# A gated decoder stack on one core: shared last feed-forward product, token shift by transfers, one barrier, gathers dealt out between scatters, merged end

## What is computed

```python
x = x + tanh(g_xattn[0]) * L0_xattn(layernorm(x), ctx)
x = x + tanh(g_ffn[0])   * L0_ffn(layernorm(x))
x = x + tanh(g_xattn[1]) * L1_xattn(layernorm(x), ctx, ctx)
x = x + tanh(g_ffn[1])   * L1_ffn(layernorm(x))

# one of the two layers of L0_ffn (HID = 682)
x = x + local_attention(shift_token(x)) @ wo
h = shift_token(x)                 # second half of the channels from the token before
h = (h - mean) / sqrt(var + 1e-5) * lg + lb
a, g = split(h @ w1 + b1)          # 682 values, 682 gates
x = x + (a * gelu(g)) @ w2 + b2

# L1_ffn, after the router has chosen idx[e], 128 tokens for each expert e
y = gelu(xe @ fc1[e].T + b) @ fc2[e].T + b2
output[idx] += y * gate;  sums[idx] += gate
output = where(sums > 0, output / sums, output)
```

## Time and profile before

| | us |
|---|---|
| median of 3 runs | 2104.79 |
| lowest, highest | 2097.73, 2105.27 |
| the profiled execution's own time | 2111.36 |
| its span, first to last instruction | 2109.6 |
| TensorE busy in it | 1819.5 (86%) |
| VectorE busy | 1278.1 (61%) |
| ScalarE busy | 1036.2 (49%) |
| GpSimd busy | 695.0 (33%) |
| mean granted clock of TensorE | 0.957 of 2.4 GHz |

### The profile page before, as it was taken

The page is one execution under the profiler, slowest core; times in us unless marked ns, Lnnn a source line. Parts: engine busy times, 40 slices in busy tenths (PEclk is TensorE's granted clock), DMA queues, the critical chain, the costliest instruction groups (busy, mean ns, idle before and its releaser), DMA issues. The chain is left out here.

```text
span 2109.6 us, 32684 instructions
## 1 busy us (share of the span) xinstructions
PE 1819.5 (86%) x11580; PEld 1199.6 (57%) x11580; DVE 1278.1 (61%) x2729; ACT 1036.2 (49%) x2194; POOL 695.0 (33%) x997
## 2 busy tenths in 40 slices
PE   6988888888799797997999989999998998870894
PEld 3455555555567466674666655466666554550794
DVE  5478888888623584233787842268876334967112
ACT  3488888888521263212767621157674111540221
POOL 0022223232332444323555521045554112450321
PEclk9999999999899999998999999999999999995897
DMA  3441111110000200021000020020000000046694
GB/s 117 158 122 41 41 42 41 41 42 2 1 0 1 60 1 1 1 61 43 1 1 1 1 62 1 0 57 1 1 1 1 0 0 16 1 146 139 198 310 134
DMA packets 99138, 99.65 MB, mean 47 GB/s; under 512 B 33740, under 2 KB 83232, under 8 KB 98848
## 3 DMA queue, kind: packets, MB, share of 16 engines
q1 hardware_dynamic: 95904, 93.21, 15.0%
q0 software_dynamic: 3072, 4.34, 1.1%
HBM read 80.60 MB, written 16.92 MB: 46 GB/s over the span
## 5 line engine op out<-in xcount | busy, mean ns | idle before, releaser
L585 DVE TENSOR_REDUCE negmax<-sps 128x1 f32<-128x1024 f32 x256 | 308.3, 1215 | 36.2 <-PE sps L530 31.0
L629 ACT ACTIVATE prob<-sps,negmax 128x1024 f32<-128x1024 f32 x256 | 287.6, 1124 | 22.2 <-DVE negmax L585 17.8
L539 PE MATMUL sps<-ident,prob 128*128 128x128 f32 x1152 | 178.3, 283 | 57.5 <-ACT prob L629 56.6
L539 PEld LDWEIGHTS sps<-ident,prob 128*128 128x128 f32 x1152 | 134.7, 143 | 142.8 <-ACT prob L629 123.0
L1491 POOL TENSOR_TENSOR la_pr<-la_pr,la_ri 128x512 f32<-128x512 f32 x128 | 157.1, 1255 | 164.2 <-DVE la_ri L1553 164.2
L674 POOL TENSOR_TENSOR probT<-probT,after 128x128 f32<-128x128 f32 x256 | 116.6, 455 | 268.4 <-DVE probT L593 192.6
L1738 ACT ACTIVATE la_pr<-la_pr,la_nx 128x256 f32<-128x256 f32 x256 | 126.3, 494 | 128.6 <-DVE la_nx L1594 128.6
L530 PE MATMUL sps<-ks,qs 128*128 128x512 f16 x512 | 162.5, 393 | 11.1 <-DVE ores L605 4.4
L1922 PE MATMUL la_bs<-lf_zT,lfw 128*128 128x512 f32 (+1 forms) x384 | 168.7, 594 | 0.0
L1501 POOL TENSOR_TENSOR la_qs<-la_qn,ores 128x256 f32<-128x256 f32 x128 | 113.6, 918 | 89.1 <-DVE la_qn L1607 89.1
L638 ACT COPY probT<-sps 128x512 f32<-128x512 f32 (+1 forms) x192 | 101.8, 530 | 40.5 <-PE sps L539 40.5
(11 more groups left out here) (384 smaller groups left out, 3808.7 us busy)
## 6 DMA issues: line engine op xcount, KB each, us to landing
w1e<-in_fc_T SPq DMA_DIRECT2D x16, 1024.0 KB, 5.6
w2e<-in_fc_T SPq DMA_DIRECT2D x16, 1024.0 KB, 8.6
qs<-q_parts SPq DMA_DIRECT2D x128, 64.0 KB, 1.9
ks<-k_parts SPq DMA_DIRECT2D x128, 64.0 KB, 2.0
q_parts<-parts SPq DMA_DIRECT2D x8, 512.0 KB, 3.7
k_parts<-parts SPq DMA_DIRECT2D x8, 512.0 KB, 3.6
ores<-in_L_ffn_wqkv SPq DMA_DIRECT2D x2, 1536.0 KB, 6.3
lfw<-in_L_ffn_w SPq DMA_DIRECT2D x2, 1364.0 KB
```

What stands on the lines that cost most here:

```text
L539: mm = pe.transpose(slots[n % 4][:, at * P:(at + 1) * P], prob[:, n % 3, t * P:(t + 1) * P], ident[:])
L585: dve.tensor_reduce(negmax[:, n % 4:n % 4 + 1], slots[n % 4][:], X, ALU.max, negate=True).then_inc(s.max_done, 1)
L629: act.activation(prob[:, n % 3, :], slots[n % 4][:], ACT.Exp, bias=negmax[:, n % 4:n % 4 + 1], accum_out=rowsum[:, tile % 2, n % QUAD:n % ...
```

## The change

1. **Last product shared.** The 42 gates and 42 values left over come from one matrix of 128 columns (values in columns 0 to 41, gates in 64 to 105, zeros between), so that chunk 5 takes two matmuls, not four. The gelu reads partitions 64 to 105 and writes 0 to 41. The weights come in 13 transfers, not 10, two of them narrow.
2. **Shift by transfers.** `late` is gone from TensorE, with `shift` and `carry`. For each group SyncE copies the half rows of x one partition down into a new SBUF tile `xs`, with two transfers after the attention has updated the group's tiles. VectorE reads `xs` from SBUF where it read PSUM. Two rows of `xs` are blanked by GpSimd at the start of the block, and VectorE waits for that before its first work (`tables`).
3. **One barrier, one release.** The four calls of `signals` end in one barrier; the five of `release` become one.
4. **Gathers dealt out.** GpSimd issues six gathers, and then one behind each of the first ten scatters.
5. **Merged end.** The end has no block: SyncE reads `mixed` as soon as the last scatter has landed, into the space of the expert weights. The divisor takes one instruction, and of each group's four result tiles the last goes to ScalarE (product) and GpSimd (sum). The semaphores are cleared behind it.

```diff
-            w1 = sb(ph + "w1", [P, KD, 2 * HID], F32, c)
+            w1 = sb(ph + "w1", [P, KD, 2 * (NF - 1) * P + P], F32, c)
...
+                for n in range(2):
+                    sp.dma_start(w1[:, :, n * full:(n + 1) * full], w1_rows[:, :, n * HID:n * HID + full]).then_inc(sem, 16)
+                with nc.allow_non_contiguous_dma(reason="the last channels of values and gates"):
+                    for n in range(2):
+                        at = 2 * full + n * P // 2
+                        sp.dma_start(w1[:, :, at:at + HID - full], w1_rows[:, :, n * HID + full:(n + 1) * HID]).then_inc(sem, 16)
...
+                            for g in range(G):
+                                t0, t1 = g * J, g * J + J
+                                sp.wait_ge(sa[l].x_done, t1)
+                                sp.dma_start(xs[1:P, t0:t1, :], x0res[0:P - 1, t0:t1, HALF:D]).then_inc(late[g], 16)
+                                if t0 % TPB == 0:
+                                    t0 += 1
+                                sp.dma_start(xs[0:1, t0:t1, :], x0res[P - 1:P, t0 - 1:t1 - 1, HALF:D]).then_inc(late[g], 16)
...
+                        for b in range(B):
+                            pool.memset(xs[0:1, b * TPB, :], 0.0).then_inc(sf[0].first_blank, 1)
...
-                                dve.tensor_scalar(z[:, j, HALF:D], tps(g)[0][:, j * P:(j + 1) * P], mom[:, j, 0:1], rs[:, j:j + 1],
+                                dve.tensor_scalar(z[:, j, HALF:D], xs[:, g * J + j, :], mom[:, j, 0:1], rs[:, j:j + 1],
...
+                            if l == 0:
+                                dve.wait_ge(w.first_blank, B)
                             tables(l)
...
-                            for dst, off in ((pg[f % 2], HID), (pa[f % 2], 0)):
+                            full = (NF - 1) * P
+                            pairs = ((pg[f % 2], full + f0), (pa[f % 2], f0)) if n == P else ((pa[f % 2], 2 * full),)
+                            for dst, at in pairs:
                                 for k in range(KD):
-                                    mm = pe.matmul(dst[0:n, :], w1[:, k, off + f0:off + f0 + n], zT[:, k, :],
-                                                   start=(k == 0), stop=(k == KD - 1))
+                                    mm = pe.matmul(dst, w1[:, k, at:at + P], zT[:, k, :], start=(k == 0), stop=(k == KD - 1))
...
-                for signals_of in sa + sf:
-                    release(signals_of)
-                release([x3_in])
+                release([signal for names in sa + sf for signal in names] + [x3_in])
...
+                    sp.wait_ge(s.added, 16 * E)
+                    for g in range(G):
+                        sp.dma_start(acc[:, g * J:(g + 1) * J, :],
+                                     mixed.rearrange("(t p) c -> p t c", p=P)[:, g * J:(g + 1) * J, :]).then_inc(mixed_in[g], 16)
+                    for g in range(G):
+                        sp.wait_ge(s.x_done, (g + 1) * (J - 1))
+                        sp.wait_ge(s.last_done, g + 1)
+                        sp.dma_start(out.rearrange("b (t p) c -> p (b t) c", p=P)[:, g * J:(g + 1) * J, :],
+                                     fin[:, g * J:(g + 1) * J, :]).then_inc(s.x_out, 16)
...
+                    for e in range(GATHERS):
+                        gather(e)
...
+                        if e + GATHERS < E:
+                            gather(e + GATHERS)
                     pool.wait_ge(s.added, 16 * E)
+                    for g in range(G):
+                        t = g * J + J - 1
+                        pool.wait_ge(s.last_scaled, g + 1)
+                        pool.tensor_tensor(fin[:, t, :], fin[:, t, :], xres[:, t, :], ALU.add).then_inc(s.last_done, 1)
```

More of the change, by code:

```diff
@@ L30, in build, with signals @@
     EPS = 1e-5
-    def signals(phase, names):
+    def signals(phase, names, last=True):
         sems = []
@@ L40, in signals @@
                 nc.gpsimd.sem_inc(sems[-1], 1)
-        nc.all_engine_barrier()
+        if last:
+            nc.all_engine_barrier()
         return namedtuple("Signals", names.replace("@", ""))(*sems)
@@ L1367, in ahead @@
                     sp.dma_start(aff[:, 1, :], chan(io["L0_ffn_ln_b"][l])).then_inc(sem, 16)
-                return 160
+                return 208
             return (w1, w2, b1, b2, aff), ahead
@@ L1466, in _ @@
                         pool.memset(hT[:, SHIFT - 1 + HB:SHIFT + HB], 0.0).then_inc(s.edges, 1)
+                        gaps = w1[:, :, 2 * (NF - 1) * P:].rearrange("p k (n c) -> p k n c", n=2)[:, :, :, HID - (NF - 1) * P:]
+                        for k in range(KD):
+                            pool.memset(gaps[:, k, :, :], 0.0).then_inc(sf[0].padded, 1)
                         pool.memset(kT[:, :, 0:P], 0.0).then_inc(s.built1, 1)
@@ L1900, in late @@
                                 pe.wait_ge(w.zT_done, g * KD)
-                            for j in range(J):
-                                t = g * J + j
-                                inner = t % TPB > 0
-                                mm = pe.matmul(tps(g)[0][:, j * P:(j + 1) * P], shift[:], x0res[:, t, HALF:D], start=True, stop=not inner)
-                                if inner:
-                                    mm = pe.matmul(tps(g)[0][:, j * P:(j + 1) * P], carry[:], x0res[:, t - 1, HALF:D], start=False, stop=True)
-                            mm.then_inc(w.late_done, 1)
-                        def turn(w, g):
                             pe.wait_ge(w.z_done, g * J + J)
@@ L1968, in _ @@
                                     hidden(w, g, f)
-                                    if f == 1 and g + 1 < G:
-                                        late(w, g + 1)
                                 for j in range(J):
@@ L1983, in build @@
         x3_ctx = ExitStack()
-        shift = sb("shift", [P, P], F32, x3_ctx)
-        carry = sb("carry", [P, P], F32, x3_ctx)
         biases3 = (io["L1_xattn_bq"], io["L1_xattn_bk"], io["L1_xattn_bv"])
@@ L2445, in weigh, with coefficients, result @@
                                           ALU.mult).then_inc(s.weighted, 1)
+                    def coefficients(g):
+                        t = slice(g * J, (g + 1) * J)
+                        dve.wait_ge(mixed_in[g], 16)
+                        dve.scalar_tensor_tensor(out=total[:, t], in0=acc[:, t, D], scalar=0.0, in1=acc[:, t, D],
+                                                 op0=ALU.is_le, op1=ALU.add).then_inc(s.total_done, 1)
+                        dve.wait_ge(s.total_done, g + 1)
+                        dve.reciprocal(coef[:, t], total[:, t]).then_inc(s.inverse_done, 1)
+                        dve.wait_ge(s.inverse_done, g + 1)
+                        dve.tensor_scalar(coef[:, t], coef[:, t], gate[:, 3:4], None, ALU.mult).then_inc(s.coef_done, 1)
+                    def result(g):
+                        dve.wait_ge(s.coef_done, g + 1)
+                        for t in range(g * J, g * J + J - 1):
+                            dve.scalar_tensor_tensor(out=fin[:, t, :], in0=acc[:, t, 0:D], scalar=coef[:, t:t + 1],
+                                                     in1=xres[:, t, :], op0=ALU.mult, op1=ALU.add).then_inc(s.x_done, 1)
                     tokens(0)
@@ L2452, in _ @@
                         weigh(e)
+                    for g in range(G):
+                        coefficients(g)
+                        result(g)
                 @block.scalar
@@ L2462, in _ @@
                         ins.then_inc(s.gelu_done, 1)
+                    for g in range(G):
+                        t = g * J + J - 1
+                        act.wait_ge(s.coef_done, g + 1)
+                        act.activation(fin[:, t, :], acc[:, t, 0:D], ACT.Copy, scale=coef[:, t:t + 1]).then_inc(s.last_scaled, 1)
                 @block.tensor
```

93 lines of the change are left out of this document (31 added, 62 removed).

## The result

The changed kernel takes 2085.31 us (median of 6, 2071.45 to 2089.86), the kernel before 2104.82 (median of 6, 2097.73 to 2105.46): a ratio of 0.991, 95% interval 0.989 to 0.993. It is faster, by 20 us where 37 were forecast, and its time lies 3.3 us above the range. Its profiled execution took 2071.45 us, against 2071.8 in the sum. So the sum holds in the trace, and what is missing lies between the traces and the timed runs.

The account below looks back on a forecast made before the run. TensorE, busy for all of 110 us at full clock, was taken to bound the feed-forwards. Gains of 39.6 us gave 2071.8 from the profiled 2111.4, or 2065.2 with the median's distance; forecast 2068 us between them, range 2058 to 2082.

Parts of the forecast that it names:

- the sum: Whole kernel: gains of 39.6 us, from the profiled 2111.4 to 2071.8 us; 2065.2 if the median's distance stays.
- shift off TensorE: Feed-forwards: 1.78 us off TensorE's path in each of six groups, 10.7 us gained; group 0 counted 0.
- shared last product: Feed-forward chunk 5: four records fewer in each of eight groups, 13.8 us, less a new wait; 12.3 us gained.
- one barrier, one release: Gaps into and out of the block: 0.9 us from three barriers, 0.4 from the releases; 1.3 us gained.
- gathers dealt: Experts' start: gathers cause TensorE's stall, 9.4 us gained, less 1 us for disturbed scatters; net 8.4 us.
- merged end: Kernel's end: 4.7 us before the read of `mixed`, 2.4 in four groups, less 0.2 for semaphores; 6.9 us gained.
- The rival of the stall: Experts' start: gathers don't cause the stall or timed runs have less of it; time 2074.6 us, chance 0.25.
- Wait for chunk 5: Feed-forwards: TensorE newly waits for VectorE's chunk 5 product, 0.25 us in six groups, 1.5 us in all.
- VectorE at group 0: Normalising from SBUF beside GpSimd's bias sums: between -0.2 and 1.4 us in a layer, taken as 0.
- The new wait of VectorE: Block's start: VectorE waits for GpSimd's blanking of `xs`; `tables` ends 1.2 us before it is wanted, cost 0.
- the rivals of the scatter chain: Experts: dealt gathers lengthen the scatter chain, moderately (2075 us, chance 0.08) or each whole (2122 us, chance 0.03).
- The last rival: More than counted: group 0's shift counts, no chunk 5 wait, undisturbed scatters; 2062 us, down to 2058, chance 0.06.

Follow-up runs that it names:

- no_transfers: Changed kernel with the shift on TensorE again instead of the transfers, the rest kept: 2087.35 us, ratio 0.989 to the kernel before.
- no_shared: Changed kernel with four matmuls for chunk 5 again, the rest kept: 2089.37 us, ratio 0.990 to the kernel before.
- only_ffn: Kernel before with only the shared last product and the shift by transfers: 2092.09 us, ratio 0.990 to the kernel before.
- four_barriers: Changed kernel with four barriers and five releases again: 2076.9 us, ratio 0.984 to the kernel before.
- gathers16: Changed kernel with all sixteen gathers first again, the rest kept: 2082.04 us, ratio 0.988 to the kernel before.

## Why the prediction was off

**The sum held.** 39.6 us were summed; the two profiled executions, at clocks of 0.957 and 0.959, differ by 39.9 us, of which about 2 us are the clock by the lines above; at equal clock all executions give 37.8. That 39.6 and 39.9 agree so closely is luck in part: some terms were too small, others too large. By its terms:

| | predicted | measured | read from |
|---|---|---|---|
| shift off TensorE | 10.7 | 11.0 | no_transfers |
| shared last product | 12.3 | 13.4 | no_shared |
| both together | 23.0 | 22.1 | only_ffn |
| one barrier, one release | 1.3 | 1.8 | gaps of 0.87 and 1.44 us for 2.1 and 1.9; 1.3 of it in four_barriers |
| gathers dealt | 8.4 | 10.0, against gathers16 8.3 | start of the stage to the issue of the last scatter: 134.9 before, 124.8 after |
| merged end | 6.9 | 5.3 | issue of the last scatter to VectorE's last instruction: 22.5 before, 17.2 after |

**The step that failed is the one from the sum to the timed runs**, in "The sum" and "How the numbers follow". I took the distance of 6.6 us between the profiled execution and the median for something that stays, and gave the range no term for the clock. The changed kernel's executions reach from 2065.4 to 2089.9 us with one text, and nearly all of that goes with the mean clock: from 0.945 to 0.962, 17 times 1.4 is 24 us, and around the line they scatter by 1 us. The first six are no exception; each lies within 1.5 us of that line. Five of them had 0.952 or less, of the nineteen later ones four. If the six were drawn at random from the 25, five or more of the nine low clocks would fall to them in about one case of 80, so something in that first comparison may have favoured low clocks; its chip is not listed, and what it was is open. Those six have a median 10.8 us above that of the later ones (2074.53). So of the 17.3 us by which the forecast of 2068 fell short, 10.8 are the low clocks of the first six, which a range up to 2082 was too narrow for. The other 6.5 us are the step down from the sum's 2071.8 to 2068 (3.8 us) and the 2.7 us by which the later median lies above 2071.8; the profiled execution had a clock of 0.959, and the line is at 2074.2 at 0.957.

The gain of 20 us in place of 37 has a second part, on the side of the kernel before, whose median the step down rested on. Its first six executions (2097.73 to 2105.46) all lie below each of the 52 later ones (2107.18 and up; median 2114.6), by some 10 us in the median. Their clocks are not listed. By the line, 2097.7 would need a clock of 0.969, which no execution had. The chip moves this kernel by 3 us at equal clock among the three known ones. The rival of the stall would explain it: executions without the stall would be some 9 us faster. But no trace of the kernel before, the first one's 2111.4 us or the two later ones (2116.48 and 2110.01), lacks it. So this part stays open: another chip, a higher clock and a missing stall are not told apart.

**Terms that were mis-sized.**

- *Shared last product.* 13.3 us for 12.3. The sum took 0.43 us for each of the four records that go, 1.72 us a group; but a group's products went from 20.82 us (48 records, no_shared) to 18.88 us (44 records), 1.94 us less. Records start 0.43 us apart, but around the change from 128 to 42 columns and at the change back it is 0.52, 0.46 and 0.52 us. Eight groups give 15.5 us, less the 2.3 us of the next point.
- *Wait for chunk 5.* The mechanism was right, 0.39 us in each of six groups, 2.3 us for the 1.5 taken. This line of the page's costliest groups has it:

```profile
L1944 PE MATMUL la_bqk<-lfw,lf_hT 128*128 128x256 f32 (+1 forms) x384 | 95.4, 392 | 2.3 <-DVE lf_hT L1663 2.3
```

- *VectorE at group 0.* "Only the first of its kind was long" was wrong, and so was the 0 for it. VectorE's timeline there:

```profile
1232.04 0.75 DVE L1653 TENSOR_SCALAR lf_z<-x0res,lf_mom,lf_rs 128x128 f32<-128x128 f32 x1 [0.19 <-POOL lf_rs L1529]
1232.71 0.77 DVE L1655 TENSOR_SCALAR lf_z<-lf_xs,lf_mom,lf_rs 128x128 f32<-128x128 f32 x1
1233.40 0.76 DVE L1653 TENSOR_SCALAR lf_z<-x0res,lf_mom,lf_rs 128x128 f32<-128x128 f32 x1
1234.09 0.76 DVE L1655 TENSOR_SCALAR lf_z<-lf_xs,lf_mom,lf_rs 128x128 f32<-128x128 f32 x1
1234.77 0.34 DVE L1653 TENSOR_SCALAR lf_z<-x0res,lf_mom,lf_rs 128x128 f32<-128x128 f32 x1
...
1231.98 2.79 POOL L1523 TENSOR_TENSOR lf_xb<-x0res,lfb 128x256 f32<-128x256 f32 x4
...
1235.93 1.09 PE L1924 MATMUL la_bqk<-ident,lf_z 128*128 128x128 f32 x8 [1.16 <-DVE lf_z L1655]
```

The four instructions that lie beside GpSimd's 2.79 us take 0.75 to 0.77 us, the next one 0.34: 1.7 us more. This is what the Trainium skill says on its page "SBUF — State Buffer", section "Who interferes with whom": a VectorE instruction in its two-port mode and a GpSimd instruction shut each other out. The estimate by that page was 5.6 us, for two layers; the rows show 1.7 for one, and the first long instruction the kernel before has too. In the kernel before, the reads of PSUM took 0.40 us beside GpSimd and without it. From the start of the first of the eight to the end of the last it is 3.84 us now and 3.14 us before (3.12 in no_transfers), 0.7 us more in either layer. In the first layer TensorE stands idle for it (1.16 us ahead of the turn, which starts 0.06 us behind VectorE's last), so 0.7 us reached the span, inside the bounds of the forecast; in the second it has other work until then. That the turn starts at 1235.93 and started at 1236.15 says nothing here, since the whole block starts 1.9 us earlier (TensorE's first record at 978.40 for 980.29).

- *The new wait of VectorE* behind GpSimd's blanking ended at 981.61, `tables` at 984.25, and 2.09 us of idle follow (the forecast left 1.2). Cost 0.

```profile
981.61 0.69 DVE L1552 TENSOR_TENSOR ores<-ores 128x512 f32<-128x512 f32 x1 [4.08 <-POOL lf_xs L1497]
...
986.34 1.22 DVE L1597 TENSOR_REDUCE la_ss<-la_sq 128x16 f32<-128x1024 f32 x1 [2.09 <-ACT la_sq L1739]
```

- *The gathers.* fc1(2) starts 3.5 us behind the end of fc1(1) and not 13.2: the stall was worth 9.6 us for the 9.4 taken. One reading behind it was wrong: landing is counted from the start of the issuing instruction, so the last gather landed at about 1968.40 + 2.9 = 1971.3, not at 1972.25, and the stall ended some 0.7 us behind that, not within 0.1 us of it. The loss of 1 us didn't come: a scatter lands in 6.3 us at the median for 6.1, the slowest in 8.0 for 8.4. The next scatter does wait for it (60.8 us of GpSimd's idle time in all, 67.4 before), but the chain got no longer: from the first scatter's issue to the last it takes 105.7 us, before 106.3. So the rivals of the scatter chain are out. (The last rival prices group 0's shift at 3.3 us where its own bound was 2 x 1.8 = 3.6; nothing hangs on it.)

```profile
DMA to landing us min/median/max: 3.7/6.3/8.0
```

- *The end.* From the last scatter's issue to the read went 4.8 us (4.7 forecast). The groups were mis-sized: one takes 2.33 us and not 2.49, all four 9.4 us and not 9.94. That is 0.5 us for the 2.4 forecast. Of the three tiles, the first two take 0.48 us each, as before, also beside ScalarE; the third, beside GpSimd's sum, takes 0.94 us. So the tile that was given away came back as a delay: GpSimd's sum is not the last work (it ends at 2065.50, VectorE's last tile at 2065.78), but it was not hidden, as the forecast had it. What is left is about the one small instruction less.

```profile
2064.03 0.51 ACT L2515 ACTIVATE x0res<-w1e,coef 128x256 f32<-128x256 f32 x1 [1.82 <-DVE coef L2485]
2064.62 0.88 POOL L2456 TENSOR_TENSOR x0res<-x0res,xres 128x256 f32<-128x256 f32 x1 [1.45 <-ACT x0res L2515]
2064.84 0.94 DVE L2490 SCALAR_TENSOR_TENSOR x0res<-w1e,coef,xres 128x256 f32<-128x256 f32 x1
```

- *SyncE's queue.* The transfers of group 3's shift were costed by a landing of 2.9 us if their cover were gone. The queue's own timeline shows more:

```profile
1239.24 0.70 SPq L1468 DMA_DIRECT2D lf_xs<-x0res  x1
1239.98 10.98 SPq L1471 DMA_DIRECT2D lf_xs<-x0res  x1
1251.01 0.45 SPq L1329 DMA_DIRECT2D ores<-in_L_ffn_wqkv  x1
```

The transfer of four short rows into one partition holds the queue for 10.98 us (all eight of its kind, 10.9 to 11.0), and layer 1's weights start 11.8 us behind the first. They are wanted at about 1366, so the cover held; but the price without it was named four times too low, and a kernel whose next load is due within 12 us would have paid it.

## What to carry to other kernels

Where one engine is busy for all of a stretch, what is taken off it leaves the span one for one, until the next engine's wait shows, and both can be read ahead of time from a trace (here 23.0 us forecast, 23.4 us in the feed-forwards). Work handed to an idle engine is not free when that engine slows the one it came from: GpSimd's fourth tile cost VectorE as much as it saved. A forecast of a timed median needs one term more: how far the mean granted clock wanders from execution to execution, here 24 us in 2075; compare kernels at equal clock, and stage by stage in the traces, before calling a missing gain a mechanism. Where a stall like this one shows, issue only as many gathers at the head of a stage as end with the work that covers them, and the rest behind the steps of the loop; six and ten did equally well here, sixteen did not.

## What the hardware showed

- The same instructions in the same order ran with 160 us or 201 us at 1.2 GHz, on one chip, in single executions: 2065.4 and 2080.5 us.
- While GpSimd issues sixteen gathers, one each 1.25 us, and for 2.4 to 2.6 us behind the last, the products behind fc1(1) start 0.7 to 1.4 us apart, where they take 0.23 us each otherwise; the same gathers beside fc1(0) and fc1(1) do nothing (8.60 us against 8.58 for 64 records).
- VectorE's `tensor_scalar` of 128 x 128 float32 from SBUF to SBUF takes 0.34 us alone and 0.75 to 0.77 us beside GpSimd's `tensor_tensor`; from PSUM it takes 0.40 us either way. Its `scalar_tensor_tensor` of 128 x 256 takes 0.48 us alone and 0.94 us beside it.
- A transfer of three or four 512-byte rows within SBUF into one partition holds SyncE's queue for 10.9 to 11.0 us; one of four such rows into each of 127 partitions for 0.70 us.
